# Slot passes of a graph network: the steps of a batch spread over more turns, four PSUM banks for the sums

## The chip, the cores and the metric

One core of one Trainium2 chip runs the whole program. Its engines are TensorE (PE, with its weight loads as PEld), VectorE (DVE), ScalarE (ACT), GpSimd (POOL) and SyncE (SP); each takes its instructions in order, and they meet at semaphores. The metric is the device time of one execution in microseconds (us).

## The reference

Four graph layers stand behind each other on 50000 nodes and 25000 edges, sorted by target node. Rows are 128 floats. After a three-layer attention network come a two-layer GCN, a one-layer GCN and a two-layer SAGE network, each with a residual and a normalisation:

```python
def sgconv_relu(h, W, b):
    msg = h[row] * norm[:, None]
    agg = jax.ops.segment_sum(msg, col, num_segments=num_nodes)
    return jax.nn.relu(agg @ W.T + b)
...
m = msg_sum / jnp.maximum(deg, 1.0)[:, None]     # SAGE
return jax.nn.relu(jnp.concatenate([h, m], axis=1) @ W + b)
...
x = _layernorm(x + L1(x)); x = _layernorm(x + L2(x)); x = _layernorm(x + L3(x))
```

## The kernel before, in words

Edges are padded to 49 batches of 4 x 128 slots; each slot holds one edge, and the last slot of a node's run stands for the node ("slot rows"). Nodes without edges have rows of their own ("node rows"). After the attention network `convolve` runs five times, as five passes over the 49 batches: passes 1 and 2 are the two GCN layers (`gcn0`, the second with residual and normalisation, `norm`), pass 3 the one-layer GCN (`norm`), passes 4 and 5 the SAGE layers (the fifth with `norm`). Pass 1 also carries 25 batches of node rows of a last layer pair (`nodes`), one beside every even batch. Pass 5 scatters its rows into the output (`placing`). A barrier ends each pass.

For a batch b of a GCN pass:

- POOL gathers the 4 x 128 source rows into `got` (L2534), four buffers deep: gather b waits until the sum of batch b - 4 is done.
- DVE builds four one-hot matrices `pick` (`build`, L2822 and L2826).
- PE sums the gathered rows through them into a PSUM bank (`sum_edges`, L2566).
- DVE carries a run that goes on from the tile before (`carry_over`, four small instructions, L1907 to L1914).
- ACT makes four diagonal matrices `own` (`diagonals`, L2696 and L2700), after a wait until the own rows of batch b - 2 were added; PE adds the batch's own rows `x` through them to the same bank (`add_own`, L2581).
- ACT copies the bank out to `agg` (`sums_out`, L2711) and puts the bias into another bank (`set_bias`, L2692); PE multiplies (`product`, L2590); DVE applies the relu and, with `norm`, adds the residual (`residual`, L2838 or L2842) and takes the moments (L2849, L2854); ACT takes the root (`deviation`, L2716), DVE inverts and scales (`scale`, L2860, L2862), ACT normalises (`normalise`, L2722); SP stores (L2494).

In a SAGE pass `add_own` is a transpose into a bank of its own (L2576), copied out by L2709, and the product has a second set of matrices (L2593).

The order on each engine is written out by hand. `skewed` calls a step function once a turn n; in it `at(k)` gives batch n - k, so that `at(2)` of turn n handles batch n - 2. `Batch.count(1, 1)` as the value of a wait means "this batch is done", `count(1, -1)` "the batch two before is done". In pass 1 of the kernel before, turn n of PE is: `sum_edges(n-1)`, node steps, `product(n-2)`, `node_turn(n-2)` if n is even, `add_own(n-1)`. Turn n of ACT is: `diagonals(n)`, node steps, `set_bias(n-1)`, `sums_out(n-1)`, and the copy `node_turned(n-2)`, L2728.

The node steps of an even batch b in pass 1 are: PE turns its rows (`node_turn`, L2602, turn b+2, after a wait until the previous node batch's middle rows were copied out of the same bank: `hold(pe, nmid_made, b.ring(1, -1))`), ACT copies (L2728), PE multiplies (`node_hidden`, L2607, turn b+3), ACT applies the relu (`node_relu`, L2733, turn b+3), PE turns back (`node_middle`, L2612, turn b+4), ACT copies out and sets a bias (`node_middle_out`, L2739 and L2741, turn b+4), PE multiplies (`node_product`, L2618, turn b+5), DVE residual and moments (L2874, L2880, L2885, turn b+5), ACT root (L2747, turn b+6), DVE scale (L2891, turn b+6), ACT normalises (`node_normalise`, L2753, turn b+7), SP stores (L2476).

Of the kernel before, what the change touches and what calls it, by code (L numbers as in the profile page):

```python
# [14 lines left out]
P = 128  # L15
# [132 lines left out]
def program(nc, io, n_nodes, n_edges):  # L148
# [5 lines left out]
    with ctx:  # L154
# [2244 lines left out]
        def convolve(n, mode, norm, t_in, t_out, t_res, weights, bias_io, nodes=None):  # L2399
# [4 lines left out]
            with ExitStack() as c, Semaphores(nc) as sem:  # L2404
# [37 lines left out]
                b_sum, b_own, b_y = bank[0:2], bank[2:4], bank[4:6]  # L2442
# [5 lines left out]
                with nc.Block() as block:  # L2448
                    @block.sync
                    def _(sp):  # L2450
# [45 lines left out]
                        def step(at):  # L2496
# [9 lines left out]
                            b = at(6 if norm else 4)  # L2506
# [8 lines left out]
                        skewed(sp, nb, 9 if nodes else 6 if norm else 4, step, 4)  # L2515
# [34 lines left out]
                    def _(pe):  # L2550
# [9 lines left out]
                        def sum_edges(b):  # L2560
# [3 lines left out]
                            hold(pe, agg_made, b.count(1, -1))  # L2564
                            for k in range(GB):
                                ins = nc.tensor.matmul(b_sum[r][:, k * P:(k + 1) * P], got[b.slot][:, k, :], pick[r][:, k, :],  # L2566
                                                       start=k == 0, stop=sage, skip_group_check=True)
                            ins.then_inc(summed, 1)

                        def add_own(b):  # L2570
# [6 lines left out]
                            else:  # L2577
                                pe.wait_ge(carry_added, b.count(1, 1))
                                pe.wait_ge(own_made, b.count(1, 1))
                                for k in range(GB):  # L2580
                                    ins = nc.tensor.matmul(b_sum[r][:, k * P:(k + 1) * P], x[b.slot][:, k, :], own[r][:, k, :],  # L2581
                                                           start=False, stop=True, skip_group_check=True)
# [50 lines left out]
                        def step_gcn_relu(at):  # L2633
# [13 lines left out]
                        def step_gcn_norm(at):  # L2647
                            b = at(2)
                            if b:
                                add_own(b)  # L2650
                            b = at(1)
                            if b:
                                sum_edges(b)
                            b = at(2)
# [3 lines left out]
                        def step_sage_relu(at):  # L2658
# [6 lines left out]
                            if b:  # L2665
                                product(b)
                            if even(b):
                                node_turn(b)

                        def step_sage_norm(at):  # L2670
# [3 lines left out]
                            b = at(0)  # L2674
                            if b:
                                add_own(b)
                            b = at(1)
                            if b:
                                sum_edges(b)
                        if sage:  # L2680
                            skewed(pe, nb, 5 if nodes else 3 if norm else 2, step_sage_norm if norm else step_sage_relu, 4)
                        else:
                            skewed(pe, nb, 5 if nodes else 2, step_gcn_norm if norm else step_gcn_relu, 4)

                    @block.scalar
                    def _(act):
# [17 lines left out]
                        def sums_out(b):  # L2704
# [6 lines left out]
                            nc.scalar.copy(flat(agg[r]), b_sum[r][:, :]).then_inc(agg_made, 1)  # L2711
# [59 lines left out]
                        def step_relu(at):  # L2771
                            b = at(0)
                            if b and not sage:
                                diagonals(b)
                            node_steps(at)
                            b = at(2 if sage else 1)
                            if b:
                                set_bias(b)
                                sums_out(b)
# [4 lines left out]
                        def step_gcn_norm(at):  # L2784
                            b = at(4)
                            if b:
                                normalise(b)
                            b = at(2)
                            if b:
                                set_bias(b)  # L2790
                                sums_out(b)
                            b = at(0)
                            if b:
                                diagonals(b)
                            b = at(3)
                            if b:
                                deviation(b)

                        def step_sage_norm(at):
                            b = at(4)  # L2800
                            if b:
                                deviation(b)
                            b = at(2)
                            if b:
                                set_bias(b)
                                sums_out(b)
                            b = at(4)
                            if b:
                                normalise(b)
                        if norm:  # L2810
                            skewed(act, nb, 4, step_sage_norm if sage else step_gcn_norm, 4)
                        else:
                            skewed(act, nb, 7 if nodes else 2 if sage else 1, step_relu, 4)

                    @block.vector
                    def _(dve):
# [48 lines left out]
                        def carry_over(b):  # L2865
                            dve.wait_ge(summed, b.count(1, 1))
                            carry(dve, b, (scanned, spread, carry_added), tails, now[b.half], carried, b_sum[b.half], dve_pace)
# [28 lines left out]
                        def step_relu(at):  # L2896
# [3 lines left out]
                            b = at(1)  # L2900
                            if b:
# [138 lines left out]
```

## Time and profile before

| | before |
|---|---|
| median of 3 runs | 5085.48 us (5083.7 to 5086.98) |
| span of the profiled execution | 5076.4 us |
| that execution from the first gather of `convolve` (3515.54) to its end | 1560.9 us |
| PE / DVE / ACT / POOL busy | 77% / 75% / 68% / 59% |

The page sums over all stages, while only `convolve` changes. So the reading goes by windows: one for each pass, cut at POOL's first gather of a pass and at the end of its last one. The first gather of the five passes starts at 3515.54, 3788.79, 4049.43, 4310.87 and 4569.90; the last gather of the first four ends at 3760.55, 4033.48, 4294.20 and 4556.56. A timeline row reads: start in us, length in us, engine, line, operation, destination and sources with the number of instructions that the row merges, and in brackets how long the engine had been idle and what ended that.

### The profile page before, as it was taken

The numbers are of one execution on the slowest core, as the hardware profiler recorded it, in microseconds if no ns is written. First come the engines' busy times: TensorE is split into PE (matmuls) and PEld (weight loads), VectorE is DVE, ScalarE is ACT, GpSimd is POOL, SyncE is SP. The second block draws the span as 40 slices with busy tenths as digits, with TensorE's granted clock in tenths as the row PEclk, the third lists the DMA queues.
The fourth block names the chain that finished last, engine by engine and source line by source line (L and its number), as shares of the span: only waits on it lengthen the run. The fifth ranks groups of instructions, "written<-read, shape, count | busy, mean of one in ns | idle before, by whom it ended". The sixth has DMA issues, their size and how long they took to land. (4 is left out here: it accounts for less than half of the span.)

```text
span 5076.4 us, 107540 instructions
## 1 busy us (share of the span) xinstructions
PE 3921.6 (77%) x23992; PEld 2865.7 (56%) x23992; DVE 3818.0 (75%) x14850; ACT 3446.1 (68%) x11317; POOL 3017.8 (59%) x2914
## 2 busy tenths in 40 slices
PE   2999999565997798994998974997876676665554
PEld 1666766344775455773555752444765565665554
DVE  5899999676998787887886966997768787444443
ACT  0899999554886576784776863887878787333332
POOL 2888888475552122661223452887757676767777
PEclk9999999788998899997999997998999898997666
DMA  2566666587997576994776984775766566543332
GB/s 63 162 186 199 199 194 193 175 288 242 351 349 250 180 239 205 338 354 160 233 241 230 350 290 156 225 227 171 230 205 212 189 204 190 155 145 116 93 101 70
DMA packets 606699, 1061.18 MB, mean 209 GB/s; under 512 B 109737, under 2 KB 130875, under 8 KB 606509
## 3 DMA queue, kind: packets, MB, share of 16 engines
q1 hardware_dynamic: 524780, 920.61, 53.0%
q0 software_dynamic: 81728, 138.51, 10.7%
q8 instruction: 61, 1.00, 0.1%
q14 instruction: 130, 1.06, 0.1%
HBM read 608.75 MB, written 453.92 MB: 209 GB/s over the span
## 5 line engine op out<-in xcount | busy, mean ns | idle before, releaser
L2534 POOL DMA_INDIRECT got_c<-table,src_row x980 | 930.4, 949 | 387.6 <-issue 295.6
L1428 POOL DMA_INDIRECT src_got_s<-table,src_row x588 | 554.6, 943 | 452.9 <-PE bank L1474 105.1
L2566 PE MATMUL bank<-pick_c,got_c 128*128 128x128 f32 x1960 | 327.7, 319 | 349.6 <-DMA got_c<-table,src_row 271.2
L2076 PE MATMUL bank<-w_all,dt_m 128*128 128x512 f32 x1176 | 567.7, 599 | 35.0 <-DMA dt_m<-delta_t 33.4
L2566 PEld LDWEIGHTS bank<-pick_c,got_c 128*128 128x128 f32 x1960 | 284.2, 223 | 392.5 <-issue 233.5
L2050 POOL TENSOR_TENSOR part_m<-part_m,half_sum_m 128x512 f32<-128x512 f32 x98 | 158.7, 1619 | 580.3 <-DVE half_sum_m L2283 580.3
L1601 ACT ACTIVATE z_s<-z_s,shift_s,dev_s 128x128 f32<-128x128 f32 x1080 | 444.2, 486 | 1.8 <-DVE shift_s L1739 1.3
L791 PEld LDWEIGHTS bank<-w_mean,ht 128*128 128x128 f32 x2352 | 312.4, 193 | 142.9 <-issue 142.9
L2590 PE MATMUL bank<-w_c,agg_c 128*128 128x128 f32 x1960 | 365.4, 311 | 5.0 <-ACT agg_c L2711 4.7
L2711 ACT COPY agg_c<-bank 128x512 f32<-128x512 f32 x245 | 142.6, 582 | 325.4 <-DVE bank L1914 277.8
L788 PE MATMUL bank<-bias,first_row 128*128 128x512 f32 x588 | 321.8, 629 | 38.7 <-ACT ht L851 13.8
L2076 PEld LDWEIGHTS bank<-w_all,dt_m 128*128 128x128 f32 x1176 | 209.5, 192 | 231.0 <-issue 132.6
L841 ACT ACTIVATE bank<-bank 128x128 f32<-128x128 f32 x1176 | 306.9, 261 | 43.9 <-PE bank L791 35.6
L2590 PEld LDWEIGHTS bank<-w_c,agg_c 128*128 128x128 f32 x1960 | 318.5, 225 | 22.3 <-issue 11.5
L2177 ACT ACTIVATE part_m<-bank,now_m 128x128 f32<-128x128 f32 x588 | 214.6, 365 | 157.6 <-PE bank L2076 142.0
L791 PE MATMUL bank<-w_mean,ht 128*128 128x128 f32 x2352 | 313.4, 277 | 0.0
L2722 ACT ACTIVATE z_c<-z_c,shift_c,dev_c 128x128 f32<-128x128 f32 x588 | 242.2, 482 | 91.0 <-DVE shift_c L2862 90.6
L739 POOL DMA_INDIRECT row_map<-node_map,slot_node x196 | 214.1, 1092 | 144.4 <-POOLq L117 91.8
L2826 DVE TENSOR_SCALAR pick_c<-iota,now_c 128x128 f32<-128x128 f32 x980 | 283.2, 366 | 10.6
L1907 DVE COPY tails_c<-tails_c 128x1 f32<-128x1 f32 x245 | 37.6, 153 | 328.6 <-PE bank L2566 323.4
L752 POOL TENSOR_TENSOR rows<-rows 128x512 f32<-128x512 f32 x196 | 260.0, 1327 | 41.1 <-DVE rows L923 38.8
L2055 POOL DMA_INDIRECT x_m<-in_x_dram,dst_node x196 | 222.1, 1133 | 98.5 <-issue 52.0
(352 smaller groups left out, 11925.4 us busy)
## 6 DMA issues: line engine op xcount, KB each, us to landing
table<-rows SPq DMA_DIRECT2D x294, 256.0 KB
x_s<-table SPq DMA_DIRECT2D x270, 256.0 KB
x_c<-table SPq DMA_DIRECT2D x245, 256.0 KB
table<-z_s SPq DMA_DIRECT2D x196, 256.0 KB
table<-z_c SPq DMA_DIRECT2D x196, 256.0 KB
table<-mid_s SPq DMA_DIRECT2D x172, 256.0 KB
own_rows_s<-table SPq DMA_DIRECT2D x147, 256.0 KB
pick_t_s<-picks_t SPq DMA_DIRECT2D x147, 256.0 KB
```

The costliest lines, as they stand in the source:

```text
L752: nc.gpsimd.tensor_tensor(flat(rows[l + 1][r]), flat(rows[l + 1][r]), flat(rows[l][r]), ALU.add).then_inc(summed[l], 1)
L788: nc.tensor.matmul(b_y[l][:, :], first_row[:, :], bias[:, l, :, :].rearrange("p g d -> p (g d)"), start=True, stop=False, skip_group_check ...
L791: ins = nc.tensor.matmul(b_y[l][:, g * D:(g + 1) * D], ht[l][b.half][:, g, :], w_mean[:, l, :], start=False, stop=True, skip_group_check=True)
L841: ins = nc.scalar.activation(bank[7][:, g * D:(g + 1) * D], b_y[l][:, g * D:(g + 1) * D], ACT.Square, accum_out=square[l][r][:, g:g + 1])
L1428: nc.gpsimd.indirect_dma_start(out=src_got[r][:, g, :], out_offset=None, in_=tables[l].rows, in_offset=bass.IndirectOffsetOnAxis(ap=src_ro ...
L1601: ins = nc.scalar.activation(v[:, g, :], v[:, g, :], ACT.Identity, bias=shift[side(b, h)][:, g:g + 1], scale=dev[side(b, h)][:, g:g + 1])
L2076: nc.tensor.matmul(b_h[k % n_h][:, :], dt[b.slot][:, k, :], w_all[:, l, :, :].rearrange("p h d -> p (h d)"), start=True, stop=True).then_i ...
L2534: nc.gpsimd.indirect_dma_start(out=got[r][:, g, :], out_offset=None, in_=t_in.rows, in_offset=bass.IndirectOffsetOnAxis(ap=src_row[:, t:t ...
L2566: ins = nc.tensor.matmul(b_sum[r][:, k * P:(k + 1) * P], got[b.slot][:, k, :], pick[r][:, k, :], start=k == 0, stop=sage, skip_group_check ...
L2590: ins = nc.tensor.matmul(b_y[r][:, k * D:(k + 1) * D], agg[r][:, k, :], ws[0][:, :], start=False, stop=True, skip_group_check=True)
L2722: ins = nc.scalar.activation(z[b.slot][:, g, :], z[b.slot][:, g, :], ACT.Identity, bias=shift[r][:, g:g + 1], scale=dev[r][:, g:g + 1])
L2826: ins = nc.vector.tensor_scalar(pick[r][:, k, :], iota[:, :], now[r][:, k, KEY:KEY + 1], now[r][:, k, COEF + m:COEF + m + 1], ALU.is_equal ...
```

## The change

It touches only `convolve`. A GCN pass sums into four banks in turn instead of two (`sum_bank`); a SAGE pass with `norm` too. The step functions of the relu and the `norm` passes become one each for GCN and SAGE, in which the parts of a batch lie a turn apart: sum in turn b+1, carry and own rows in b+2, copy out and product in b+3, residual in b+4, scale in b+5, normalise in b+6, store in b+8 (b+6 without `norm`). In a SAGE pass the copy out is in b+2. The node steps keep their turns. `deviation` gets a wait for `z_made` of the batch two before.

```diff
-                b_sum, b_own, b_y = bank[0:2], bank[2:4], bank[4:6]
+                b_own, b_y = bank[2:4], bank[4:6]
+                b_sum = bank[0:4] if not sage else bank[0:2] if nodes else bank[0:2] + bank[6:8]
+                n_sum = len(b_sum)
...
-                            b = at(6 if norm else 4)
+                            b = at(8 if norm else 6)
                             if b and not placing:
                                 store(b)
...
-                            hold(pe, agg_made, b.count(1, -1))
+                            hold(pe, agg_made, b.count(1, 1 - n_sum))
...
-                        def step_gcn_relu(at):
+                        def step_gcn(at):
                             b = at(1)
                             if b:
                                 sum_edges(b)
                             node_steps(at)
                             b = at(2)
                             if b:
-                                product(b)
+                                add_own(b)
                             if even(b):
                                 node_turn(b)
-                            b = at(1)
-                            if b:
-                                add_own(b)
-
...
+                            b = at(3)
                             if b:
                                 product(b)
...
+                            hold(act, z_made, b.count(1, -1))
...
-                        def step_relu(at):
-                            b = at(0)
-                            if b and not sage:
+                        def step_gcn(at):
+                            b = at(3)
+                            if b:
+                                sums_out(b)
+                            b = at(6)
+                            if b and norm:
+                                normalise(b)
+                            b = at(0)
+                            if b:
                                 diagonals(b)
+                            b = at(2)
+                            if b:
+                                set_bias(b)
+                            b = at(4)
+                            if b and norm:
+                                deviation(b)
                             node_steps(at)
...
                             b = at(2)
                             if even(b):
                                 node_turned(b)
...
+                        def step(at):
+                            b = at(2)
+                            if b:
+                                carry_over(b)
+                            b = at(5)
+                            if b and norm:
+                                scale(b)
+                            b = at(4)
+                            if b:
+                                residual(b)
+                            if b and norm:
+                                moments(b)
                             b = at(0)
                             if b:
                                 build(b)
...
```

In the new pass 1 turn n of PE is `sum_edges(n-1)`, node steps, `add_own(n-2)`, `node_turn(n-2)` if n is even, `product(n-3)`. In a SAGE pass it is `add_own(n-1)`, `sum_edges(n-1)`, `product(n-3)`.

## Rows read from the trace of the kernel before

**Rows 1.** Windows of passes 1, 3 and 5: engines' busy us, granted clock, DMA share, GB/s

```profile
3515.54:3760.55 245.01, 207.65 (x1543) 180.41 (x1544) 165.78 (x714) 201.92 (x532) 185.55 (x196) 0.98 0.73 226
...
4049.43:4294.20 244.77, 167.92 (x1137) 151.37 (x1138) 191.93 (x942) 202.67 (x568) 185.32 (x196) 0.90 0.66 207
...
4569.90:5076.40 506.50, 281.36 (x1376) 268.00 (x1376) 201.59 (x979) 172.54 (x392) 381.18 (x392) 0.68 0.32 95
```

**Rows 2.** Timeline of POOL, first gather of pass 2

```profile
3788.79 0.94 POOL L2534 DMA_INDIRECT got_c<-table,src_row  x1 [28.25 <-POOLq L117]
```

**Rows 3.** Timeline of ACT in the middle of pass 1, from a node relu on

```profile
3647.51 0.69 ACT L2733 ACTIVATE nht_c<-bank,nb_c 128x512 f32<-128x512 f32 x1
...
3649.64 0.57 ACT L2692 COPY bank<-bias_c 128x512 f32<-128x512 f32 x1
...
3650.15 0.58 ACT L2711 COPY agg_c<-bank 128x512 f32<-128x512 f32 x1
...
3650.89 1.28 ACT L2700 ACTIVATE own_c<-ident,now_own_c 128x128 f32<-128x128 f32 x4
...
3652.07 0.56 ACT L2739 COPY nmid_c<-bank 128x512 f32<-128x512 f32 x1
```

**Rows 4.** Timeline of PE's weight loads there, with the ACT copy that waits

```profile
3643.27 0.42 PEld L2602 LDWEIGHTS bank<-ident,nx_c 128*128 128x128 f32 x4 [1.31 <-DMA nx_c<-table]
...
3643.66 0.97 PEld L2581 LDWEIGHTS bank<-own_c,x_c 128*128 128x128 f32 x8
...
3644.55 0.97 PEld L2566 LDWEIGHTS bank<-pick_c,got_c 128*128 128x128 f32 x8
...
3644.86 0.58 ACT L2711 COPY agg_c<-bank 128x512 f32<-128x512 f32 x1 [0.73 <-PE bank L2581]
...
3646.34 0.30 PEld L2607 LDWEIGHTS bank<-nxt_c,nw_c 128*128 128x128 f32 x2
...
3647.31 0.86 PEld L2590 LDWEIGHTS bank<-w_c,agg_c 128*128 128x128 f32 x7 [0.24 <-issue]
```

**Rows 5.** Timeline there: issue of a node load, and PE's node turn after it

```profile
3649.94 0.35 SPq L2464 DMA_DIRECT2D nx_c<-table  x1
...
3653.02 0.66 PE L2602 MATMUL bank<-ident,nx_c 128*128 128x128 f32 x4 [1.09 <-DMA nx_c<-table]
```

**Rows 6.** Timeline of PE at the start of pass 1, sum of batch 2

```profile
3533.28 1.16 PE L2566 MATMUL bank<-pick_c,got_c 128*128 128x128 f32 x8 [0.85 <-DMA got_c<-table,src_row]
```

**Rows 7.** Timeline of PE at the end of pass 1, last own rows (batch 48)

```profile
3767.48 1.06 PE L2581 MATMUL bank<-own_c,x_c 128*128 128x128 f32 x8
```

**Rows 8.** Timeline at the end of pass 2: last two residuals, last normalisation

```profile
4037.97 0.69 DVE L2842 SCALAR_TENSOR_TENSOR z_c<-bank,res_c 128x512 f32<-128x512 f32 x1 [0.35 <-PE bank L2590]
...
4040.91 0.69 DVE L2842 SCALAR_TENSOR_TENSOR z_c<-bank,res_c 128x512 f32<-128x512 f32 x1
...
4043.81 1.65 ACT L2722 ACTIVATE z_c<-z_c,shift_c,dev_c 128x128 f32<-128x128 f32 x4 [0.44 <-DVE shift_c L2862]
```

**Rows 9.** Timeline of DVE at the end of pass 4: last two residuals

```profile
4563.32 0.69 DVE L2838 TENSOR_SCALAR z_c<-bank 128x512 f32<-128x512 f32 x1 [2.66 <-PE bank L2593]
...
4565.17 0.69 DVE L2838 TENSOR_SCALAR z_c<-bank 128x512 f32<-128x512 f32 x1 [1.16 <-PE bank L2593]
```

**Rows 10.** Timeline at the end of pass 5: a root on ACT, a scatter on POOL

```profile
5049.67 0.30 ACT L2716 ACTIVATE dev_c<-stat_c,eps 128x4 f32<-128x4 f32 x1 [2.87 <-DVE stat_c L2854]
...
5050.10 0.97 POOL L2542 DMA_INDIRECT out_dram<-z_c,slot_node  x1 [0.30 <-issue]
```

**Rows 11.** Timeline in the middle of pass 2: a residual and the store after it

```profile
4019.28 0.68 DVE L2842 SCALAR_TENSOR_TENSOR z_c<-bank,res_c 128x512 f32<-128x512 f32 x1
...
4020.48 0.37 SPq L2494 DMA_DIRECT2D table<-z_c  x1
```

**Rows 12.** Timeline at the end of pass 1: a node store, and the residual after it

```profile
3769.99 0.36 SPq L2476 DMA_DIRECT2D out_dram<-nz_c  x1
...
3774.88 0.69 DVE L2874 SCALAR_TENSOR_TENSOR nz_c<-bank,nx_c 128x512 f32<-128x512 f32 x1 [2.65 <-DMA out_dram<-nz_c]
```

More of the change, by code:

```diff
@@ L2514, in step @@
                                 store_nodes(b)
-                        skewed(sp, nb, 9 if nodes else 6 if norm else 4, step, 4)
+                        skewed(sp, nb, 9 if nodes else 8 if norm else 6, step, 4)
                         if nodes:
@@ L2580, in add_own @@
                                 for k in range(GB):
-                                    ins = nc.tensor.matmul(b_sum[r][:, k * P:(k + 1) * P], x[b.slot][:, k, :], own[r][:, k, :],
+                                    ins = nc.tensor.matmul(sum_bank(b)[:, k * P:(k + 1) * P], x[b.slot][:, k, :], own[r][:, k, :],
                                                            start=False, stop=True, skip_group_check=True)
@@ L2673, in step_sage_norm @@
                                 product(b)
-                            b = at(0)
[L2675 to L2683, printed above, removed]
+                        skewed(pe, nb, 5 if nodes else 3, step_sage if sage else step_gcn, 4)
                     @block.scalar
@@ L2710, in sums_out @@
                                 act.wait_ge(carry_added, b.count(1, 1))
[L2711 removed]
+                            nc.scalar.copy(flat(agg[r]), sum_bank(b)[:, :]).then_inc(agg_made, 1)
                         def deviation(b):
@@ L2789, in step_gcn_norm @@
                             if b:
+                                sums_out(b)
                                 set_bias(b)
[L2791 to L2796, printed above, removed]
+                            b = at(4)
+                            if b and norm:
                                 deviation(b)
[L2799 to L2802, printed above, removed]
+                            node_steps(at)
                             b = at(2)
[L2804 to L2813, printed above, removed]
+                            if even(b):
+                                node_turned(b)
+                        skewed(act, nb, 7 if nodes else 6 if norm else 3, step_sage if sage else step_gcn, 4)
                     @block.vector
@@ L2866, in carry_over @@
                             dve.wait_ge(summed, b.count(1, 1))
-                            carry(dve, b, (scanned, spread, carry_added), tails, now[b.half], carried, b_sum[b.half], dve_pace)
+                            carry(dve, b, (scanned, spread, carry_added), tails, now[b.half], carried, sum_bank(b), dve_pace)
                         def node_residual(b):
@@ L2912, in step_relu @@
                                 node_moments(b)
-                        def step_gcn_norm(at):
-                            b = at(2)
-                            if b:
-                                carry_over(b)
-                            b = at(0)
-                            if b:
-                                build(b)
-                            b = at(3)
-                            if b:
-                                residual(b)
-                                moments(b)
-                                scale(b)
-                        def step_sage_norm(at):
-                            b = at(4)
-                            if b:
-                                moments(b)
-                            b = at(2)
-                            if b:
-                                carry_over(b)
-                            b = at(0)
-                            if b:
-                                build(b)
-                            b = at(4)
-                            if b:
-                                scale(b)
-                            b = at(3)
-                            if b:
-                                residual(b)
-                        if norm:
-                            skewed(dve, nb, 4 if sage else 3, step_sage_norm if sage else step_gcn_norm, 4)
-                        else:
-                            skewed(dve, nb, 6 if nodes else 2, step_relu, 4)
+                            b = at(6)
+                            if even(b):
+                                node_scale(b)
+                        skewed(dve, nb, 6 if nodes else 5 if norm else 4, step, 4)
         t = tables + [final]
```

39 lines of the change are left out of this document (10 added, 29 removed).

## The prediction, made before the changed kernel was run

> **What bounds the kernel now.** I read the windows first, one for each pass, because the page's shares are averages over stages that the change does not touch. In each window the reader is to compare POOL's count with the length. Pass 1 has 196 gathers in 245.01 us and pass 3 has 196 in 244.77 us, 1.25 us for each, although the two passes have quite different work on DVE and PE; pass 5 has 392 gathers and scatters in 506.5 us, 1.29 for each [rows 1]. POOL issues without a break, so POOL's list of indirect DMAs sets the length of every pass: 5.0 us for a batch, 10.0 for two, and 10.3 for a batch in pass 5. A faster or smoother order on PE, ACT and DVE is worth nothing there. What the others add is the drain, from the last gather of a pass to the first of the next: 28.2 us after pass 1 [rows 1, 2], about 16 after each of the `norm` passes. So a change of order can win only in the drains, and it can lose in two places: in the drains, or where a new chain of waits is longer than POOL's 10.0 us for two batches.
>
> The second view is the timeline of two turns in the middle of pass 1, the fullest pass: ACT is busy 201.92 of 245.01 us and PE 207.65 [rows 1]. I looked there for the loop of waits that comes back to itself. It goes from the node relu over ACT's queue to the copy of the middle rows, which ends at 3652.63, 5.12 us after the relu's start [rows 3]; then over PE's queue to the hidden product, and back to the relu. The kernel before takes on PE: node turn, own rows, sum, node product, hidden product. From the loads that is 0.39 + 0.89 + 1.79 [rows 4], and some 1.2 for the hidden product and two hand-overs, 4.3 in all: a loop of 9.4 us, less than 10.0. Beside it the node load adds 1.09 us of waiting at the turn [rows 5]; POOL still does not wait.
>
> **The change, part by part.** Nothing is computed more or less: the instructions are the same, and they are reordered. The four banks let a sum start without the copy-out of the batch two before; PE's sums follow their gathers anyway and POOL is not held, so this is worth nothing in time. The new wait in `deviation` is for a normalisation that stands earlier in ACT's own queue: nothing.
>
> *Pass 1, the main term.* `add_own` of batch n-2 now stands in PE's turn n, and ACT's `diagonals(n)`, in the same turn n, still waits for just this batch (the buffer `own` has two halves). Before, that batch had been added a turn earlier. What is queued behind `diagonals` on ACT is the bias, and then every node step: the relu, or the copy of the middle rows. And PE's `node_turn(n-2)` waits for that copy, with `product(n-3)` and the next turn's sum, node product, hidden product and own rows queued behind it. So the two engines now take turns instead of overlapping. The loop for two turns, from rows: from the copy's end PE gets the word in 0.04; node turn 0.39 (3643.27 to 3643.66); slot product 0.89, taken like the own rows, which have the same eight loads (3643.66 to 3644.55); sum and node product 1.79 (3644.55 to 3646.34); hidden product 0.97 (3646.34 to 3647.31); own rows until ACT starts 1.20 (3643.66 to 3644.86) [rows 4]. Then on ACT four diagonals 1.18 and the bias 0.51 [rows 3]. That is 6.97. Then the relu, the node normalisation, the copy-out, the next diagonals, the bias and the middle copy, the same set as before and 5.12 in all [rows 3]; the second diagonals' own wait is over by then. Sum: 12.1 us for two turns against POOL's 10.0. POOL's ring of four buffers gives slack once and no more. The pass is then set by PE and ACT, and POOL stands and waits for sums.
>
> The length: the sum of batch 2 starts at 3533.28 [rows 6] and is early enough to stay there; the own rows of turn 3 end 0.89 + 0.97 + 1.16 later, 3536.3. To turn 49 there are 23 loops. In the first two there is no node normalisation yet, 1.55 less (four normalising instructions take 1.65 [rows 8], of which 0.1 lies under the next instruction). 21 x 12.1 + 2 x 10.55 = 275.2, so the own rows of batch 47 end at 3811.5. From there to the next pass: before, the last own rows ended at 3768.54 and the next pass's gather came at 3788.79, 20.3 us [rows 7, 2]; the own rows of batch 47 stand one turn ahead of the last ones, but in the drain there are no more diagonals, so I add 1.0: 21.3. The next pass starts at 3832.8 instead of 3788.79: +44.0 us. An error of 0.4 in the loop would be 9 us, so this term goes from 35 to 53.
>
> *Passes 2 and 3.* No node steps here, and each engine's turn rests on the turn before; the longest loop that I find (carry, own rows, diagonals, bias, root, scale, residual, moments, build) takes about 7.6 us for two turns. POOL goes on. The drain gets longer. When the last sum ends, three batches are still ahead of their residuals instead of two. Before, the residuals of 47 and 48 start at 4037.97 and 4040.91, 2.94 apart, and the last normalisation runs 4043.81 to 4045.46 [rows 8]. Now the one at 4037.97 is batch 46's, that of 48 starts at 4043.85, its root is at 4046.0; ACT has the normalisation of 47 behind that root, to 4047.8, and that of 48 ends at 4049.4. +3.9 us, for each of the two passes; 2.9 if the normalisations overlap better. 7.8 in all.
>
> *Pass 4.* The last sum is followed by three products instead of two. One takes 1.85 us at the high clock [rows 9], up to about 3.5 at the low one: +2.0.
>
> *Pass 5.* POOL's scatter of batch 45 starts at 5050.10. The new order has the normalisation of 45 behind the root of 46, and that root falls where a root falls now, at 5049.67, since it hangs on the first product after the last sum [rows 10]. 5049.67 + 0.2 + 1.65 = 5051.5, so POOL waits 1.4 us, once. Later batches are in time. +1.4.
>
> *Sum.* 44.0 + 7.8 + 2.0 + 1.4 = 55.2 us. The profiled execution would have a span of 5076.4 + 55.2 = 5131.6; the runs' median lies 9.1 above that execution's span, so 5085.48 + 55.2 = 5140.7.
>
> **Rivals.** *A, the loop of pass 1 stays covered (not slower).* This is the other side. It decides at a loop of 10.0 us: if ACT's diagonals did not have to wait in the same turn, or if PE reached the own rows early, the loop would be the old 9.4. For it speaks that both engines are only 82% and 85% busy [rows 1]; against it that each link is a wait written in the code, in queues that keep their order. Then pass 1 even gains: in the drain the node residual of batch 44 no longer stands behind the carry of 48 and the product and residual of 47 (0.7 + 0.89 + 0.69, with the node groups between them an estimated 3.7 us), and the sum is -3.7 + 7.8 + 2.0 + 1.4 = +7.5: 5093.
>
> *B, PE's clock falls in pass 1.* With the longer loop PE is busy 207.65 / (245 + 44) = 72%, against 85%. Pass 3 has PE busy for 69% and a granted clock of 0.90, pass 5 56% and 0.68 [rows 1]; a clock of 0.90 is a fifth of the time at 1.2 GHz. The six PE groups of the loop are 5.2 us, so at 0.90 the loop grows by 1.0: +24, 5165. At half of that, 5153. The Trainium skill, "TensorE: Matmul & The Clock Gate", under "What's actually happening", says that the throttled state is the default and activity releases it, so that a PE which now waits for ACT in every second turn would be slowed on top; the rows of passes 1 and 3 agree in direction.
>
> *C, the stores of passes 2 and 3 become a loop.* `store` moves to turn b+8, and in SP's queue of that turn it stands behind a load that waits for the residual of batch b+3; the residual of batch b+4, next on DVE, waits for that store's landing. One turn of this loop is 1.20 us from residual to store issue [rows 11], plus the landing. As far as rows go, a load of the same size landed in 3.1 us in full traffic [rows 5], and a store in 4.9 with others around it [rows 12]: 4.3 to 6.1, against 5.0. At 4.3 it costs nothing; at 5.2 it is 0.2 x 96 = +19 us (5160), at 6.1 over +100. I take the load's, because the traffic in passes 2 and 3 is lower (0.66 against 0.73 [rows 1]). The Trainium skill, "DMA: Bandwidth & Descriptors", under "Anatomy of one DMA", gives a fixed 2.0 us plus bytes over 436 GB/s, an estimate of 2.6 us for 256 KB and a loop of 3.8; the rows have longer landings, so it speaks for no cost but not strongly.
>
> *D, nothing of the drains shows and pass 1 gains its 3.7.* 5082, about no change or a hair faster.
>
> **How the numbers follow.** Forecast 0.64, at 5140.7. B 0.14, C 0.09, A 0.10, D 0.03. The forecast's own range is 5131 to 5151, from the bounds of the loop. The range for 8 in 10 goes from 5120, for a loop of 11.2, to 5172, which takes in B and the low part of C; A, D and the rest of C are left out. What can be told from no change is about 0.2%, 10 us. Faster by more: 0.02; within: 0.10 (A and D); slower: 0.88.
>
> **What would show it.** Pass 1 must be longer: POOL's rows in its middle must have waits for the sums (L2566), 196 gathers in about 285 us instead of 245, and the hidden product must come back every 12.1 us. ACT's diagonals must start right behind PE's own rows, with some 3 us of idle time before them in every second turn. Passes 2 to 4 must keep 245 us for their 196 gathers, with drains longer by 3.9, 3.9 and 2. Pass 5 must keep 10.2 us for a batch, with one wait of POOL near its end. Wrong would be: pass 1 at 245 us (A); slots in pass 1 with a clock under 0.95 (B); DVE waiting for `z_c` stores in passes 2 and 3 (C).

## The result, and the profile after

The changed kernel takes 5179.26 us (median of 4 runs, 5177.47 to 5206.43), the kernel before 5085.48. The ratio over all runs is 1.0196, with a 95% interval of 1.018 to 1.0211; the two medians by themselves give 1.0184, because one run took 5206 us and the other three 5177 to 5181. Ratios below are also taken over all runs. The sign and the place were as forecast, the size was not: +94 us against a forecast of +55, and 7 us above the end of the range.

The profiled execution has a span of 5175.4 us, 99.0 more than before. The windows of the changed kernel are cut as in [rows 1], at POOL's first gather of a pass and at the end of its last one, and give pass 1, its drain, pass 2, its drain, pass 4 and pass 5. The columns are the same: length, busy us of PE, PEld, DVE, ACT and POOL, the granted clock, DMA share, GB/s.

```profile
3516.85:3824.79 307.94, 219.88 (x1454) 199.00 (x1454) 159.43 (x684) 188.08 (x499) 185.87 (x196) 0.88 0.56 173
3824.79:3869.66 44.87, 26.54 (x178) 23.72 (x178) 19.04 (x86) 28.42 (x71) 0.00 (x1) 0.82 0.38 132
3869.66:4115.06 245.40, 175.24 (x1131) 163.40 (x1132) 183.47 (x916) 188.69 (x550) 185.93 (x196) 0.83 0.68 201
4115.06:4137.91 22.85, 7.88 (x52) 7.30 (x50) 12.40 (x67) 15.27 (x40) 0.00 (x1) 0.74 0.29 107
...
4406.26:4652.17 245.91, 166.60 (x1320) 153.89 (x1320) 121.12 (x482) 74.17 (x142) 186.44 (x196) 0.97 0.51 154
...
4667.57:5175.42 507.85, 242.35 (x1376) 228.71 (x1376) 201.44 (x979) 168.92 (x392) 381.62 (x392) 0.76 0.32 95
```

| from first gather to first gather of the next | before | after | difference | forecast |
|---|---|---|---|---|
| pass 1 | 273.3 | 352.8 | +79.6 | +44.0 |
| pass 2 | 260.6 | 268.3 | +7.6 | +3.9 |
| pass 3 | 261.4 | 268.4 | +6.9 | +3.9 |
| pass 4 | 259.0 | 261.3 | +2.3 | +2.0 |
| pass 5, to the end | 506.5 | 507.9 | +1.3 | +1.4 |

The first gather of pass 1 itself lies 1.3 us later (3516.85); what is ahead of it is the same code, and from kernel to kernel this point moved by some us (3515.2 to 3522.2 on the chips with the same pace), so that the windows say more than the spans. The waits in pass 1 of the changed kernel (who waited for what: us in total, times, longest) name the loop that the prediction wrote down:

```profile
ACT own_c L2681 <- PE bank L2586: 100.0, 25, 4.9
...
PEld bank L2607 <- issue: 69.2, 22, 3.2
POOL got_c L2539 <- PE bank L2571: 67.5, 17, 4.2
PE bank L2607 <- ACT nmid_c L2721: 65.6, 22, 3.1
```

ACT's diagonals wait for PE's own rows, 25 times, 4 us each; PE's node turn waits for ACT's middle copy, 22 times, 3 us each; and POOL, which in the kernel before stood no longer between two gathers of pass 1 than the usual 0.3 us, waits 67.5 us for the sums. The timeline of one round in the middle of the pass shows the size:

```profile
3692.23 0.58 ACT L2721 COPY nmid_c<-bank 128x512 f32<-128x512 f32 x1
...
3692.92 0.71 PEld L2607 LDWEIGHTS bank<-ident,nx_c 128*128 128x128 f32 x4 [3.15 <-issue]
3692.95 1.08 PE L2607 MATMUL bank<-ident,nx_c 128*128 128x128 f32 x4 [2.99 <-ACT nmid_c L2721]
...
3693.62 1.83 PEld L2595 LDWEIGHTS bank<-w_c,agg_c 128*128 128x128 f32 x8
...
3695.33 1.36 PEld L2571 LDWEIGHTS bank<-pick_c,got_c 128*128 128x128 f32 x8
...
3696.61 0.97 PEld L2623 LDWEIGHTS bank<-nw_c,nht_c 128*128 128x128 f32 x8
...
3697.16 0.94 POOL L2539 DMA_INDIRECT got_c<-table,src_row  x1 [3.72 <-PE bank L2571]
...
3699.62 1.28 ACT L2681 ACTIVATE own_c<-ident,now_own_c 128x128 f32<-128x128 f32 x4 [4.35 <-PE bank L2586]
...
3701.33 0.68 ACT L2715 ACTIVATE nht_c<-bank,nb_c 128x512 f32<-128x512 f32 x1
...
3706.65 0.71 PEld L2607 LDWEIGHTS bank<-ident,nx_c 128*128 128x128 f32 x4 [3.23 <-issue]
```

From node turn to node turn it is 3706.65 - 3692.92 = 13.7 us, not 12.1. The order of events is the forecast one. The difference stands in three rows behind PE's gap of 3 us: the node turn's loads take 0.71 instead of 0.42, the product's 1.83 instead of 0.97 and the sum's 1.36 instead of 0.97, and only the node product at 3696.61 is back at 0.97. By their starts these three steps take 0.70 + 1.71 + 1.28 = 3.69 us against 0.39 + 0.89 + 0.89 = 2.17 in [rows 4]: 1.52 us in this round. That is TensorE at 1.2 GHz behind its gap, and back at 2.4 GHz by the node product; the pass's granted clock is 0.88.

The slow stretch does not always start with the node turn. In the earlier rounds of the pass it sets in behind it and reaches into the node product:

```profile
3568.85 0.42 PEld L2607 LDWEIGHTS bank<-ident,nx_c 128*128 128x128 f32 x4 [3.15 <-issue]
3569.24 1.27 PEld L2595 LDWEIGHTS bank<-w_c,agg_c 128*128 128x128 f32 x8
3570.39 1.83 PEld L2571 LDWEIGHTS bank<-pick_c,got_c 128*128 128x128 f32 x8
3572.10 1.53 PEld L2623 LDWEIGHTS bank<-nw_c,nht_c 128*128 128x128 f32 x8
3573.55 0.30 PEld L2612 LDWEIGHTS bank<-nxt_c,nw_c 128*128 128x128 f32 x2
```

Here product, sum and node product take 4.31 us by their starts instead of 3 x 0.89, so 1.64 us are lost. By the same reading each of the 22 rounds from 3555.09 on loses 1.47 to 1.64 us, and the round at 3543.43 ahead of them loses nothing.

### The profile page after: what moved, and what is told of

Its sections match the earlier page's. It is cut to its first block and busy times, and to the rows that moved or that the text cites. A ratio compares the mean times of both kernels' runs of the same rounds, so it can differ in the third digit from the quotient of the medians.

```text
span 5175.4 us, 107739 instructions
## 1 busy us (share of the span) xinstructions
PE 3935.8 (76%) x23992; PEld 2892.7 (56%) x23992; DVE 3809.4 (74%) x14850; ACT 3428.0 (66%) x11317; POOL 3026.1 (58%) x2914
## 5 line engine op out<-in xcount | busy, mean ns | idle before, releaser
L2571 PE MATMUL bank<-pick_c,got_c 128*128 128x128 f32 x1960 | 344.1, 331 | 460.0 <-DMA got_c<-table,src_row 328.9
L2571 PEld LDWEIGHTS bank<-pick_c,got_c 128*128 128x128 f32 x1960 | 299.2, 233 | 504.2 <-issue 287.7
L2690 ACT COPY own_c<-bank 128x512 f32<-128x512 f32 x98 | 57.5, 587 | 449.6 <-PE bank L2598 433.3
L2595 PEld LDWEIGHTS bank<-w_c,agg_c 128*128 128x128 f32 x1960 | 331.4, 236 | 3.5 <-ACT agg_c L2692 2.7
L2681 ACT ACTIVATE own_c<-ident,now_own_c 128x128 f32<-128x128 f32 x588 | 188.5, 392 | 206.2 <-PE bank L2586 202.8
```

The costliest lines, as they stand in the source:

```text
L2571: ins = nc.tensor.matmul(sum_bank(b)[:, k * P:(k + 1) * P], got[b.slot][:, k, :], pick[r][:, k, :], start=k == 0, stop=sage, skip_group_ch ...
L2595: ins = nc.tensor.matmul(b_y[r][:, k * D:(k + 1) * D], agg[r][:, k, :], ws[0][:, :], start=False, stop=True, skip_group_check=True)
```

## The experiments

Five groups. The first two ask where the loss is, the next two what opens the loop, the rest what the clock and the banks are worth.

**Pass 1 alone, and all but pass 1.** In `p1_only` only pass 1 is new; `p1_old` is the converse. Both contain the step functions of both kernels and choose by pass:

```diff
+                old = not nodes          # p1_only; p1_old: old = bool(nodes)
+                if old:
+                    b_sum = bank[0:2]
...
-                        skewed(pe, nb, 5 if nodes else 3, step_sage if sage else step_gcn, 4)
+                        if not old:
+                            skewed(pe, nb, 5 if nodes else 3, step_sage if sage else step_gcn, 4)
+                        elif sage:
+                            skewed(pe, nb, 5 if nodes else 3 if norm else 2, step_sage_norm if norm else step_sage_relu, 4)
+                        else:
+                            skewed(pe, nb, 5 if nodes else 2, step_gcn_norm if norm else step_gcn_relu, 4)
```

> Only pass 1 takes the new order, the four sum banks and the later store; passes 2 to 5 keep the old step functions, two banks and the old store turn. Theory (the diagonals' wait for own rows of the same turn puts PE and ACT in series, and PE's clock falls in the gap): pass 1 with its drain is 79.6 us longer (352.8 against 273.3), all others as before, 5165 us. Rival (the loss comes from the wider spread as such and is shared by all passes): well under 5165, about 5120.

> The converse: pass 1 keeps the old order, two banks and the old store turn, passes 2 to 5 are new. Theory: pass 1 is back at 245.0 plus 28.2 us; what is left are the longer drains of passes 2, 3 and 4 and the one wait in pass 5, by the changed kernel's trace 7.6 + 6.9 + 2.3 + 1.4 = 18: 5104 us. Rival (new orders in the other passes are harmless or good): 5086 or less.

Measured: `p1_only` 5165.06 us, 1.0161 of before (1.0144 to 1.0178); `p1_old` 5098.16 us, 1.0029 (1.0019 to 1.004). Pass 1 and its drain in the windows of `p1_only`, then pass 2 of the same kernel, in the old order:

```profile
3519.96:3832.84 312.88, 225.54 (x1454) 203.36 (x1454) 159.00 (x684) 187.69 (x499) 185.20 (x196) 0.86 0.55 170
3832.84:3877.75 44.91, 26.59 (x178) 23.75 (x178) 19.05 (x85) 28.39 (x71) 0.00 (x0) 0.82 0.38 131
3877.75:4122.69 244.94, 166.79 (x1148) 149.87 (x1148) 192.13 (x945) 203.14 (x570) 185.51 (x196) 0.92 0.67 207
4122.69:4138.68 15.99, 4.28 (x32) 3.80 (x32) 6.97 (x39) 7.68 (x20) 0.00 (x2) 0.86 0.19 71
```

So the loss splits: four fifths or more in pass 1, nearly all of the rest in longer drains. In `p1_old` pass 1 took 245.34 + 29.37 us, and the drains of passes 2 and 3 were 22.7 and 23.1 us. Its total is 6 us under the expectation. Its drain of pass 4 was 13.8 instead of the changed kernel's 15.4, and the kernel before took 1.6 us less beside it; where the rest went is not shown.

**Opening the loop, two ways.** `own4` gives the diagonals four buffers in the GCN passes; no order is changed:

```diff
+                own = pairs("own") if sage else [s(f"own{r}", [P, GB, D]) for r in range(4)]
...
-                            hold(act, own_added, b.count(1, -1))
+                            hold(act, own_added, b.count(1, -3))
```

> The changed kernel with four buffers for the diagonals in GCN passes, and the wait of the diagonals set two batches further back; every order is the new one. Theory: the loop of pass 1 opens, POOL sets its pace again, 196 gathers in 245 us, and its drain is some 4 us shorter than before: 5104 - 4 = 5100 us, with the hidden product back every 10.0 us. Rival (PE's lower clock is the cause and the wait only its companion): pass 1 stays at 290 us or more, and the whole above 5140.

`act_order` changes no buffer and no wait, only what is queued behind the wait:

```diff
                             if b and norm:
                                 normalise(b)
+                            node_steps(at)
                             b = at(0)
                             if b:
                                 diagonals(b)
...
-                            node_steps(at)
```

> The changed kernel with one move on ACT: node steps stand ahead of the diagonals in a turn, so that the copy of the middle rows is no longer queued behind the diagonals' wait; buffers and waits stay. Theory: the loop is the old 9.4 us, pass 1 at 245 us, the whole 5100 us. Rival (it is the wait itself and not what is queued behind it): pass 1 stays long, 5150 us or more.

Measured: `own4` 5095.32 us, 1.0034 of before (1.002 to 1.0048); `act_order` 5095.87 us, 1.0019 (1.0008 to 1.003). Pass 1 and its drain, first in `own4`, then in `act_order`:

```profile
3516.41:3761.47 245.06, 200.93 (x1529) 179.77 (x1530) 166.89 (x717) 201.41 (x531) 185.62 (x196) 0.96 0.71 226
3761.47:3788.27 26.80, 14.14 (x106) 12.05 (x104) 11.52 (x53) 16.63 (x39) 0.01 (x2) 0.83 0.40 141
```

```profile
3522.20:3767.27 245.07, 201.55 (x1530) 180.24 (x1531) 167.19 (x717) 197.20 (x526) 185.64 (x196) 0.96 0.71 226
3767.27:3793.90 26.63, 13.97 (x104) 11.90 (x103) 11.52 (x53) 18.21 (x45) 0.00 (x2) 0.84 0.40 142
```

Each takes one link out of the loop, and the pass is back at POOL's 245 us; the clock comes back with it, to 0.96. The node turns of `own4` come every 9.9 us in the mean (without the first interval), and wait for their own load again, as before the change:

```profile
3693.69 0.42 PEld L2608 LDWEIGHTS bank<-ident,nx_c 128*128 128x128 f32 x4 [1.65 <-DMA nx_c<-table]
...
3703.25 0.42 PEld L2608 LDWEIGHTS bank<-ident,nx_c 128*128 128x128 f32 x4 [1.54 <-DMA nx_c<-table]
```

The drain of pass 1 is some 1.5 us shorter than before, not the 3.7 of rival A. The lower clock cannot have been the first cause: it went away when only the loop was opened.

**The clock's share.** The clock can be touched too: PE is given throwaway work in the gap. The work needs a bank that nobody reads. With two sum banks one is free, so `two_banks` was run beside it.

```diff
-                b_sum = bank[0:4] if not sage else bank[0:2] if nodes else bank[0:2] + bank[6:8]
+                b_sum = bank[0:2]                # two_banks, filler
...
                             if even(b):
+                                for k in range(12):      # filler
+                                    nc.tensor.matmul(bank[3][:, k % GB * P:(k % GB + 1) * P], ident[:, :], ident[:, :],
+                                                     start=True, stop=True, skip_group_check=True)
                                 node_turn(b)
```

> The changed kernel with two sum banks in every pass instead of four. Theory: the banks are worth nothing, since POOL or the loop sets the pace: 5179 us, pass 1 with its drain at 353 us. Rival (the two extra banks are what the spread order lives on): the sums wait for the copy-out a turn later, pass 1 longer than 360 us and waits of POOL in pass 2 too.

> Two sum banks, and in every even turn of pass 1 twelve more 128 x 128 matmuls on PE, ahead of its wait for the middle copy, into a bank that nobody reads. They take about 2.7 us at 2.4 GHz of a gap of 3.1 us, and leave PE busy there. Theory (the gap costs once by its length and once more by the clock that is low after it, 13.7 us for a loop of 12.1): the loop falls to 12.1 us although PE has more to do, pass 1 with its drain from 353 to about 316, the whole 5142 us. Rival (the clock follows the mean load or costs nothing): 5179 us or more.

Measured: `two_banks` 5281.16 us (two runs), 1.0387 of before (1.0368 to 1.0406), and `filler` 5243.44 us, 1.0314 (1.0299 to 1.033). Both expectations are missed: 5281 for 5179, and 5243 for 5142. The rival of the first came true. With two banks the sum of batch n-1 waits for the copy-out of n-3, which ACT makes in the same turn; the timeline of `two_banks` around an even turn of pass 1:

```profile
3699.78 1.64 ACT L2735 ACTIVATE nz_c<-nz_c,nshift_c,ndev_c 128x128 f32<-128x128 f32 x4
3701.31 0.56 ACT L2692 COPY agg_c<-bank 128x512 f32<-128x512 f32 x1
3701.78 0.23 ACT L2677 COPY now_own_c<-meta 128x48 f32 x1
3701.93 1.56 PEld L2571 LDWEIGHTS bank<-pick_c,got_c 128*128 128x128 f32 x8 [3.83 <-ACT agg_c L2692]
```

PE now waits a second time in each round, 3.8 us, for ACT's normalisation and the copy behind it, and its granted clock in pass 1 is 0.76. The statement of the prediction that four banks are worth nothing is false in the closed loop. The filler was worth 37.7 us beside `two_banks`, with a granted clock of 0.90 in pass 1. That is about the 37 that were expected, but from another base. So the pair was repeated with four banks, the filler going to the sum bank that is free in that turn:

```diff
                             if even(b):
+                                for k in range(12):
+                                    nc.tensor.matmul(b_sum[(b.slot + 2) % 4][:, k % GB * P:(k % GB + 1) * P], ident[:, :], ident[:, :],
+                                                     start=True, stop=True, skip_group_check=True)
                                 node_turn(b)
```

> The changed kernel with its four sum banks, and in every even turn of pass 1 twelve more 128 x 128 matmuls on PE ahead of its wait for the middle copy, into the sum bank that is free in that turn (2.7 us of a gap of 3.1). Nothing else differs. Theory (of the 3.7 us by which the loop exceeds POOL's 10.0, 2.1 are the waits in series and 1.6 the low clock after the gap): the loop is 12.1 us, pass 1 with its drain falls from 353 to about 316, the whole 5142 us. Rival (the two-bank run showed an effect of the second gap only): 5170 us or more.

> The changed kernel with four buffers for the diagonals and only two sum banks in every pass. Theory (the banks matter only while the loop of pass 1 is closed, since then a second wait, sum for copy-out, opens a second gap; with the loop open POOL sets the pace): as own4, 5095 us, pass 1 at 245. Rival (the spread order needs four banks by itself): pass 1 over 250 us, 5110 or more.

These two ran on another chip, on which the kernel before takes 5639 us: `filler4` 5661.31, 1.0047 of before there (1.0032 to 1.0061), `own4_two` 5652.89, 1.0024 (1.0011 to 1.0038). There POOL needs 300 us for the 196 gathers of pass 1, so 12.2 us for two turns instead of 10.0. A longer idle time stands ahead of the first gather of every batch, as in `own4_two`:

```profile
3853.80 0.95 POOL L2540 DMA_INDIRECT got_c<-table,src_row  x1 [1.41 <-PE bank L2572]
3855.05 0.94 POOL L2540 DMA_INDIRECT got_c<-table,src_row  x1 [0.30 <-issue]
```

The releaser named there changes from batch to batch, so the rows do not show what POOL waits for. A pace of 12.2 us covers a loop of 12.1. Only a run of the changed kernel beside the filler could tell:

> The changed kernel itself, beside the next run on the same chip, because the last two runs stood on a chip on which the kernel before takes 5639 us and POOL's gathers come 1.5 us apart, slower than the loop. Expected where the kernel before takes about 5085: 5179 us, a loop of 13.7 us, pass 1 with its drain at 353 us. Where it takes about 5640, POOL gives 12.2 us for two turns and the loop of 13.7 is only 1.5 above: pass 1 and drain about 35 us above the 337 us of own4_two.

> The kernel of the run filler4 again (four sum banks, twelve more matmuls in PE's gap of every even turn). Theory as there: where the kernel before takes about 5085, a loop of 12.1 us and 37 us less than the changed kernel, 5142; where it takes about 5640, the loop of 12.1 is just covered by POOL's 12.2, and the gain over the changed kernel is about 30. Rival: no gain over the changed kernel beside it.

Measured on a third chip, with a kernel before of 5640.23 and the same slow pace: the changed kernel 5697.35 us, 1.0097 (1.008 to 1.0113), and with the filler 5661.68, 1.0038 (1.0023 to 1.0052). Twelve matmuls more in every second turn make it 35.7 us faster. Pass 1 with its drain takes 373.9 us in `after_again`, 36.8 above `own4_two` as expected, and 343.7 in `filler4_again`: 30.2 us less. A further 4 us of the difference lie ahead of pass 1, where both run the same code. The node turns in `after_again`, 13.6 us apart:

```profile
3889.69 0.72 PEld L2607 LDWEIGHTS bank<-ident,nx_c 128*128 128x128 f32 x4 [3.22 <-issue]
3903.30 0.72 PEld L2607 LDWEIGHTS bank<-ident,nx_c 128*128 128x128 f32 x4 [3.14 <-issue]
```

and in `filler4_again`, 12.4 apart, with loads of 0.42:

```profile
3883.24 0.42 PEld L2607 LDWEIGHTS bank<-ident,nx_c 128*128 128x128 f32 x4 [0.47 <-issue]
3895.65 0.42 PEld L2607 LDWEIGHTS bank<-ident,nx_c 128*128 128x128 f32 x4 [0.55 <-issue]
```

and 200 us of pass 1 in each of them, `after_again` first:

```profile
3760.00:3960.00 200.00, 144.17 (x957) 132.21 (x956) 104.39 (x452) 128.20 (x339) 111.76 (x118) 0.87 0.55 174
```

```profile
3760.00:3960.00 200.00, 182.28 (x1458) 167.16 (x1456) 114.27 (x502) 139.34 (x368) 122.59 (x129) 1.00 0.62 191
```

Granted clock 0.87 against 1.00. The part of the low clock is shown: some 30 us of pass 1 there, where POOL's own pace cuts the gain. At a pace of 10.0 us for two turns it was shown only with two banks (`filler`). `own4_two` answers the question on the banks as far as that chip can: with the loop open two banks keep pass 1 at POOL's pace (299.9 us against 300.5 in `filler4_again`), although its sums still wait for copy-outs. At a gather pace of 10.0 us for two turns it was not tried.

**The drains, and a better version.** `own4_prod` is `own4` with the product moved ahead of the sum in passes 2 to 5:

```diff
                         def step_gcn(at):
+                            b = at(3)
+                            if b and norm:
+                                product(b)
                             b = at(1)
                             if b:
...
                             b = at(3)
-                            if b:
+                            if b and not norm:
                                 product(b)
...
```

> Four buffers for the diagonals as in the run own4, and in the four passes after the first PE takes the product of the batch three back before the sum of the newest instead of after it. Theory (the longer drains are work that is queued behind the last gather): the product, and with it the residual of batch 46, is out of the drain: passes 2 and 3 drain in about 19.8 us instead of 22.0, pass 4 in 12 instead of 13.8, so 5095 - 6 = 5089 us. Rival (the drain is set by three residuals on DVE behind the last carry, wherever the product is): drains stay at 22, 5095 us.

Measured: 5091.2 us, 1.0015 of before (1.0005 to 1.0024). Its drains of passes 2, 3 and 4 (in `own4` 22.0, 22.0 and 13.8 us):

```profile
4033.13:4053.90 20.77, 6.98 (x54) 6.05 (x52) 11.20 (x60) 14.33 (x38) 0.00 (x0) 0.84 0.29 107
4299.09:4319.40 20.31, 6.39 (x48) 5.63 (x48) 10.17 (x51) 12.52 (x33) 0.00 (x0) 0.77 0.24 92
4564.32:4576.98 12.66, 5.11 (x42) 4.62 (x40) 3.19 (x11) 1.96 (x4) 0.00 (x1) 0.97 0.24 88
```

1.3, 1.7 and 1.1 us shorter, two thirds of what was expected; the larger part of the longer drain, about 4 us, is there whatever the product's place. The gain is small against how far these drains scatter with unchanged code: the new drains of passes 2 and 3 took 21.5 to 23.1 us in `after`, `own4`, `p1_old` and `act_order`, the old ones 16.0 to 17.7 in `before`, `p1_only` and `best`. The intervals of `own4` and `own4_prod` overlap as well, so the product's part is likely rather than shown. `best` joins what was good: pass 1 new with four buffers for the diagonals, the other passes old.

> Pass 1 in the new order with four buffers for the diagonals, passes 2 to 5 in the old order. Theory: every pass at POOL's pace, the drain of pass 1 at 26.8 us instead of 28.2, the others at 16: 1.5 us less than before, 5082.5 us, no difference that can be told from zero. Rival (some of the new order's cost is outside the drains): 5090 us or more.

Measured: 5082.77 us, 0.9997 of before (0.9988 to 1.0006), no difference. Pass 1 took 245.00 + 26.91 us there. None of the versions is faster than the kernel before.

## Why the prediction was wrong, point by point

- *What bounds the kernel before*: right. With the loop open in four kernels (`p1_old`, `own4`, `act_order`, `best`) passes 1 to 4 stay between 244.8 and 245.5 us, whatever the order on PE, ACT and DVE.
- *The loop of pass 1*: the mechanism was right in each link, and so were its waits; the term of the sum was mis-sized. 6.97 + 5.12 = 12.1 was worked out with loads at 2.4 GHz, from a stretch of the kernel before in which PE never waited for 3 us. The step that failed is that the new wait on PE was priced by its length alone, with the groups behind it at their full speed: node turn, product and sum stand in the sum at 0.39 + 0.89 + 0.89 = 2.17 us and took 3.69. Taking this 1.52 out of the measured 13.7 leaves 12.2. The gap itself was in the sum: behind the relu, which starts at 6.97, PE has some 0.69 + 0.39 + 0.97 us until its own rows are done, so it is ready at 9.0, and the middle copy is done at 12.1.
- With the low clock added, the forecast for pass 1 would have been close, but partly by luck. The 21 rounds from 3555.09 to 3843.14 took 13.72 us each, 34 us more than 21 x 12.1. The two rounds ahead of them, which were put at 10.55 without the node normalisation, took 13.49 and 11.66, 4 us more, and the start and the way to the next pass were 2.4 us shorter than forecast: 44.0 + 34.0 + 4.0 - 2.4 = 79.6. The second of these two ran wholly at the full clock and was still 1.1 above its 10.55; why was not followed.
- *Rival B* had the right cause, and its sign, a clock under 0.95 in pass 1, was seen (0.88). But it spread a clock of 0.90 evenly over the loop (1.0 a round, +24) and was given 0.14. Gap and slow groups are one event, and its price was 1.5 to 1.6 a round.
- The Trainium skill, "TensorE: Matmul & The Clock Gate", under "HAM oscillation", tells of a kernel in which every group of matmuls waits for a transfer and then starts at the low clock. The trace agrees in that each of the 22 rounds from 3555.09 on has its slow stretch behind its gap. It differs in where the stretch starts: the same four loads take 0.71 instead of 0.42 us in the middle of the pass, but still 0.42 in the earlier rounds, where the groups after them are the slow ones.
- *Banks*: wrong as a general statement. They save 102 us in the closed loop; that two are enough in the open one is shown only at the slower gather pace. (By the code, both SAGE passes have four sum banks after the change, not only the one with `norm`.)
- *Passes 2 and 3*: +7.6 and +6.9 instead of +3.9 each. The trace of the changed kernel at the end of pass 2 has the last sum at 4118.04, and then

```profile
4118.93 1.40 PEld L2586 LDWEIGHTS bank<-own_c,x_c 128*128 128x128 f32 x8
...
4120.21 1.83 PEld L2595 LDWEIGHTS bank<-w_c,agg_c 128*128 128x128 f32 x8
...
4122.51 0.69 DVE L2818 SCALAR_TENSOR_TENSOR z_c<-bank,res_c 128x512 f32<-128x512 f32 x1 [1.66 <-PE bank L2595]
...
4125.45 0.69 DVE L2818 SCALAR_TENSOR_TENSOR z_c<-bank,res_c 128x512 f32<-128x512 f32 x1
...
4128.39 0.69 DVE L2818 SCALAR_TENSOR_TENSOR z_c<-bank,res_c 128x512 f32<-128x512 f32 x1
...
4130.76 3.18 ACT L2704 ACTIVATE z_c<-z_c,shift_c,dev_c 128x128 f32<-128x128 f32 x8
```

  The three residuals 2.94 apart and the two normalisations behind the last root are the forecast, 3.9 us. What I left out: the last sum starts 3.0 us behind the last gather instead of 2.2, and the first of the three residuals starts 4.47 us behind that sum instead of 2.24. In this trace it waits for its product, which stands on PE behind the own rows, both slow (1.40 and 1.83 us for eight loads). That makes 0.72 + 2.23 + 3.94 = 6.9 us more of drain in pass 2; the 196 gathers took 0.7 more as well, 7.6 in all. The low clock is not needed for it: in `own4` the loads behind the last sum took 0.97 and the drain was 22.0 us all the same, with the last sum 3.5 us behind the last gather. What sets these parts stays open.
- *Pass 4*: +2.3 for +2.0, but not more than an agreement within the scatter. The same new code had a drain of 13.7 or 13.8 us in `own4`, `p1_old` and `act_order` and 15.4 here; the old code had 13.3 in two kernels and 11.7 in `p1_only`.
- *Pass 5*: +1.3 for +1.4, and POOL had its one wait for a normalisation near the end, but a shorter one than forecast:

```profile
5149.04 0.97 POOL L2547 DMA_INDIRECT out_dram<-z_c,slot_node  x1 [0.90 <-ACT z_c L2704]
```

  0.90 instead of the usual 0.30 us is 0.6 of the 1.4; the other 0.7 came up elsewhere in the pass. The sum is right in part by luck.
- *Rival C*: its sign was seen too. DVE did wait for the stores, 16.8 us in 32 waits in pass 2, none longer than some 1 us, and the pass kept its 245.4 us; at these stores the loop costs nothing that shows. The estimate from the Trainium skill, "DMA: Bandwidth & Descriptors", under "Anatomy of one DMA", is the page's fit for transfers that GpSimd issues, and these stores are issued by SyncE, so it bears on them loosely. *Rival A*: excluded by the waits.
- *The range*: it reached to 5172, for a clock of 0.90. With the low clock in the loop priced as above (+34 to 35) it would have been centred at about 5175. The chances do not quite add up: A and D together are 0.13, while 0.10 is given for no difference and 0.02 for faster.

## What to carry to other kernels

Before a step is moved a turn, write down for each wait whether what it waits for is now made in the same turn, and what is queued behind it on both engines: two such waits that face each other put two engines in series, and a loop that was covered before can then become what sets the pace. A new wait of some microseconds on TensorE can cost its length and the low clock of the groups behind it, here half as much again (3.0 and 1.5 us); price both together. The deeper pipeline cost at most 1 us in the steady state of passes 2 to 4 and some 6 us in each drain of passes 2 and 3, so it should be this deep only where something waits.

## What the runs showed of the hardware that was not expected

Twelve more fp32 matmuls of 128 x 128 in a gap of PE made the same kernel 36 us faster, 30 of it in the pass that has them, where the granted clock was 1.00 instead of 0.87. Behind a gap of 3 us the slow stretch began with the node turn in some rounds and about 1 us later, in the product, in others, and cost 1.5 to 1.6 us either way. And the pace of the gathers differed with the chip: with the loop open, the 196 gathers of pass 1 took 245 us on some chips and 300 on another (`own4_two`), with about 1.1 us more than usual ahead of every fourth; the gathers of passes 2 and 3 took 299 to 308 us there and on a further chip. Why is not shown. The loop of waits costs 81 us in pass 1 and its drain at the first pace (against `own4`), and 37 at the second (against `own4_two`).
